# A prefetch hint on the closing branch of the loops of a one-core, eight-layer kernel

## What is computed

```python
x = L0_attn_x
x = _layernorm(x + _L0_attn_ref(x, ...))   # a recurrent cell over 1024 steps: "cells" in the kernel
x = _layernorm(x + _L0_ffn_ref(x, ...))
x = _layernorm(x + _L1_attn_ref(x, ...))
x = _layernorm(x + _L1_ffn_ref(x, ...))
x = _layernorm(x + _L2_attn_ref(x, ...))
x = _layernorm(x + _L2_ffn_ref(x, ...))
x = _layernorm(x + _L3_attn_ref(x, ...))
x = _layernorm(x + _L3_ffn_ref(x, ...))    # six blocks of local attention and a gated FFN: "local"
```

```python
retrieved = jnp.einsum('bnij,bnj->bni', S, kn)
delta = v_t - retrieved
outer = delta[..., :, None] * kn[..., None, :]
S_upd = jnp.tanh(beta_t[..., None] * S + outer)
S_new = (1.0 - w) * S + w * S_upd
```

## Time and profile before

| | |
|---|---|
| median of 3 runs | 8015.45 us (8005.39 to 8021.79) |
| the profiled execution | 8023.4 us, its span 8021.6 us |
| TensorE busy | 6678.4 us (83%) |
| VectorE busy | 6026.7 us (75%) |
| GpSimd busy | 3689.6 us (46%) |
| ScalarE busy | 2874.5 us (36%) |

### The profile page before, as it was taken

How to read it: one execution, slowest core, us unless ns; L and a number is a source line. 1 busy time by engine, 2 the same in 40 slices (tenths; PEclk the granted TensorE clock), 3 DMA queues, 4 the chain that set the end, 5 groups by cost and what they waited for, 6 DMA issues and landing times. The chain is left out here.

```text
span 8021.6 us, 237061 instructions
## 1 busy us (share of the span) xinstructions
PE 6678.4 (83%) x89269; PEld 3954.0 (49%) x89449; DVE 6026.7 (75%) x12205; ACT 2874.5 (36%) x5767; POOL 3689.6 (46%) x4646
## 2 busy tenths in 40 slices
PE   4888888888875655787876999999999999999997
PEld 2666666666631222252443554555555455555543
DVE  7777777777767668786874877777777777777776
ACT  2111111111134232313223555455554555555554
POOL 0333333333300000110302777777777777777774
PEclk7999999999987877988987999999999999999999
DMA  0000000000000000000003222222222222222222
GB/s 21 1 1 0 1 1 0 1 0 1 0 6 1 1 14 0 0 1 0 1 1 113 74 70 71 71 70 79 68 74 73 71 71 73 71 71 74 68 71 73
DMA packets 213313, 292.27 MB, mean 36 GB/s; under 512 B 27872, under 2 KB 193280, under 8 KB 206592
## 3 DMA queue, kind: packets, MB, share of 16 engines
q1 hardware_dynamic: 212224, 277.76, 11.6%
HBM read 235.94 MB, written 13.66 MB: 31 GB/s over the span
## 5 line engine op out<-in xcount | busy, mean ns | idle before, releaser
L2917 POOL TENSOR_TENSOR big<-big 128x512 f32<-128x512 f32 x776 | 1076.3, 1413 | 68.8 <-DMA big<-norms 57.6
L836 POOL TENSOR_TENSOR big<-big 128x128 f32<-128x128 f32 x1024 | 415.2, 405 | 1275.1 <-DVE big L782 1274.8
L2272 PE MATMUL banks<-hidden,big 128*128 128x256 f32 x3104 | 800.2, 402 | 120.1 <-DVE big L2741 49.7
L600 ACT ACTIVATE banks<-banks 128x128 f32<-128x128 f32 x1024 | 268.3, 262 | 1759.0 <-DVE banks L763 1759.0
L1956 POOL TENSOR_TENSOR big<-big 128x448 f32<-128x448 f32 (+10 forms) x160 | 142.5, 891 | 1618.7 <-DVE weights_odd L1820 1546.8
L2334 PE MATMUL banks<-big,hidden 128*32 128x512 f32 x6144 | 791.8, 611 | 0.0
L489 PE MATMUL banks<-big 128*128 128x256 f32 x2050 | 727.3, 437 | 60.8 <-ACT big L574 59.4
L2272 PEld LDWEIGHTS banks<-hidden,big 128*128 128x128 f32 x3104 | 580.4, 196 | 383.9 <-DVE big L2741 141.4
L2313 PE MATMUL banks<-big 32*32 32x64 f32 (+1 forms) x49152 | 599.6, 224 | 199.3 <-issue 199.0
L2313 PEld LDWEIGHTS banks<-big 32*32 32x32 f32 x49152 | 517.7, 104 | 437.2 <-issue 436.5
L334 PE MATMUL banks<-big,weights_even 128*128 128x512 f32 (+5 forms) x1056 | 499.5, 668 | 249.2 <-DVE big L1088 45.1
(11 more groups left out here) (360 smaller groups left out, 14046.4 us busy)
## 6 DMA issues: line engine op xcount, KB each, us to landing
big<-norms SPq DMA_DIRECT2D x776, 128.0 KB, 3.0
big<-qk SPq DMA_DIRECT2D x50, 512.0 KB, 4.6
big<-vo SPq DMA_DIRECT2D x25, 1024.0 KB, 5.7
small<-tables SPq DMA_DIRECT2D x196, 128.0 KB, 2.3
weights_odd<-ffn SPq DMA_DIRECT2D x25, 537.5 KB, 5.8
big<-tables SPq DMA_DIRECT2D x98, 128.0 KB, 2.2
weights_even<-tables SPq DMA_DIRECT2D x98, 128.0 KB, 2.9
hidden<-big SPq DMA_DIRECT2D x171, 64.0 KB, 2.4
```

The costliest lines, as they stand in the source:

```text
L836: nc.gpsimd.tensor_tensor(full(u["kS"][s % 2]), full(S), by(u["ko_c"]), ALU.mult).then_inc(*e.did(("kS", s)))
L2272: mm = self.nc.tensor.matmul(bank[:, n * QTOK:(n + 1) * QTOK], u["w" + name.lower()][:, (2 * g + n) * P:(2 * g + n + 1) * P], u["xs"][:, a ...
L2917: self.nc.gpsimd.tensor_tensor(x, x, u["norms"][:, n, g].unsqueeze(1).broadcast_to([P, 2, QTOK]), ALU.mult).then_inc(*e.did(("scaled", f, ...
```

## The change

`_Turns` opens its loop through the whole-core object instead of the engine, for the same one engine, and asks for a hint on the branch that closes it.

```diff
     def __enter__(self):
-        self.fori, self.base = self.engine.eng.Fori(0, self.count), [e.n for e in self.counted]
+        eng = self.engine.eng
+        self.fori = eng.bass.Fori(0, self.count, engines=[eng.engine], hint_back_edge=True)
+        self.base = [e.n for e in self.counted]
         at = self.fori.__enter__()
         for e in self.counted:
             e.loops[self.loop] = at
```

## The result

The changed kernel takes 7970.97 us (median of 5 runs, 7969.44 to 7975.0) against 8015.45 us (5 runs, 8005.39 to 8025.13): a ratio of 0.9945, 95% interval 0.9931 to 0.9960, so about 44 us less. The forecast was 7974.0. The sum that led to it contains one term that is too large, one that is at the wrong place, and it lacks one that is worth nearly a third of the gain.

A forecast was written before the change was run, and what follows sets the result against it. VectorE's code fetch at the loop's head, 2.8 us a branch, was taken as the bound. 36.3 + 6.4 - 1.3 = 41.4 us saved takes 8015.45 to 7974.0 us; own range 7953 to 7994, for 8 in 10 up to 8020.

The forecast's parts named there:

- What bounds it: At VectorE's loop heads: code fetch costs 2.8 us per branch; in the time loop all 2.9 us are on the path.
- Time loop, VectorE: VectorE's 15 time loop branches: 0.43 us of each 2.85 us gap stays, 2.42 is saved, 36.3 us in all.
- The other engines in the time loop: ScalarE, TensorE and GpSimd in the time loop: their hint is covered by the wait for the next step's data, cost 0.
- Turns: 23 branches of the loop over turns: VectorE starts at most 0.74 us earlier, 0.28 reach TensorE, 6.4 us saved.
- Ends of the loops: Behind the time loop's untaken last branch: code may be missing, VectorE's first operation late; 1.3 us lost, ends 0 and 3.
- Rival 1: Both loops: the hint, given a whole pass before the branch, does nothing; 8016 to 8021 us, say 8017; chance 0.15.
- Rival 2: TensorE's scores: the head's packet delays its code, 1.13 us per wait; 8098 us if at all 110; chance 0.09.
- Rival 3: Behind the loop's head: following code is missing, VectorE stops a little later, half the gain goes; 7995 us; chance 0.05.

## Why the prediction was right, point by point

**What bounds it.** Right: VectorE's wait ahead of line 760 was code, and the time loop's branch was where the gain lay. The late hints show it best: same hint, same branch, and without the head's packet in time the 2.8 us come back.

**Time loop, VectorE: the term of 36.3 us was 33.5.** 0.43 us were to stay of each gap, and 0.62 stayed (0.68 at the branch shown above). The hint costs 0.07 (0.11 was taken, the lower end was 0.06). What was too small is the 0.25 us for a branch that finds its code, taken from ScalarE: from the end of VectorE's branch to its next instruction it is 0.47 us in the time loop. In the turns it is 0.19 us, and with the branch's own 0.06 that is the 0.25 supposed. The two loops differ in that the time loop's code is fetched again on every pass (7 packets), while in the turns there is no 8 KB packet at all; that this is the reason is not shown.

**What was not in the sum: 13 us of TensorE's clock.** This is the step that failed. The earlier trace rows were read up to the first step behind the branch, 1.96 us, and taken to show that nothing else hangs on the gap. The next two steps, 2.43 and 2.34 us, were not looked at, nor the granted clock around the branch. What the removed wait gave was here over a third more than the wait (46.6 us in place of 33.5).

**The other engines in the time loop: 0.** Right within the interval, by the kernel with VectorE's hint alone.

**Turns.** In mechanism right, in size nearly: 0.23 instead of 0.28 us a turn, 5.3 instead of 6.4 us. The rotation was to start at the square's end, and starts 0.23 us later, so it gained 0.53, not 0.74. The 16 us by which the turns got shorter in the profiled pair can't all be put down to the hint: turns without it took 147.65 to 148.72 us in six profiles, with it 147.36 to 148.11 in eight. The means, 148.26 and 147.78, are 0.48 us apart, 11 us in all, but the kernel with the hint in the turns alone leaves room for 7 us at most.

**Ends of the loops.** 1.3 us (0 to 3) were put at VectorE's first operation behind the loop. That one starts 1.87 us behind the branch in both profiles, so the code right behind the branch is not missing, and the mechanism of this term was wrong. The price is 2.7 us and falls 35 us later; by the packets VectorE enters there a block that was not fetched. That 2.7 lies within the ends is luck.

The parts as measured, 33.5 + 13.1 + 5.3 - 2.7 = 49.2 us, stand against 48.4 us in the profiled pair and 44.5 us in the medians. The profiled pair differs in parts that the sum doesn't hold, too: the stretch between the loops grew by 10.8 us more than the 2.7, and the turns shrank by 10.8 us more than the 5.3, and the two cancel. That the forecast of 41.4 us came so near is in part luck: the missing 13.1 us were covered by smaller misses of the other sign (2.8, 1.1 and 1.4 us) and by the spread of the stretches that the hint doesn't touch.

**Rivals.** Rival 1, the hint does nothing, is what happens with the hint at step 60 or later. But its argument was the wrong way round. It feared that a hint a whole pass ahead is forgotten, and it is the near one that fails. The Trainium skill, page "Runtime: NRT & Kernel Launch", section "Instruction fetch mechanics", on which it leant, says "Prefetch is purely sequential". The traces agree for VectorE's branches of the time loop without a hint in time (8 packets a pass, 2.8 us), and differ under the hint (7 packets, 0.47 us). Rival 2 did not come: TensorE's issue waits in the scores are 104 with 191.8 us. Rival 3 did not come behind the head, as the three issue waits of VectorE that are left in the list (1.3 us together) stand elsewhere and were there before; behind the last pass its mechanism is what the 2.7 us are.

## What to carry to other kernels

A wait in front of a loop's first instruction that no semaphore explains was here a wait for code, and a hint on the closing branch took most of it away when it was given well ahead: the head of the pass or six short steps ahead of the branch were early enough, four steps or less were too late. Look at the engine on the path first: the same hint on the other engines was worth nothing that could be measured. And before a wait is priced, read the granted clock and the next few steps behind it, since an engine that idles through the wait may pay once more afterwards.

## What the runs showed of the hardware beside that

- The hint doesn't start a fetch by itself; it seems to change what the next regular packet brings. Given 11.9 us ahead it acted, given 7.9 us ahead it didn't, with that packet 8.2 us ahead.
- Under the hint a shorter body seems to stay on the engine. Between the first and the last branch of the turns the kernel before moved 228 packets of 8 KB, the one with the hint on VectorE alone 114, the changed one none, though the code is the same. VectorE's body has some 380 instructions there. In the time loop it has 780, and that one goes on being fetched.
- A hinted branch that falls through had a price in the time loop, and it came late: 2.7 us, 35 us behind the branch, in all five profiles where the hint acted there and in none of the nine others.
- TensorE's granted clock fell behind a pause of 3 us in a stream that was otherwise steady (1.00, then 0.54 and 0.61 in windows of 2 us). With the pause cut to 1.7 to 2.0 us it fell in 9 passes of 15, with the pause filled in none.
